# Attention of a 16-head language-model layer on one core: key projections one head ahead, a head finished at the end of the next one, fewer lower halves on VectorE, outputs read one unit later

## What is computed

```python
q = concat([q_nope, rope(q_rope)])                      # from nq = rms(x @ w_cq)
a1 = attn(q, k1, v1, causal=True)                       # LATENT: keys from ckv
a2 = attn(q, ks, vs, causal=False)                      # SELECT: 64 selected tokens
kw = (x @ w_wink); kw = concat([kw[:NOPE], rope(kw[NOPE:])])
a3 = attn(q, kw, vw, causal=True)                       # WINDOW
out = (g0 * a1 + g1 * a2 + g2 * a3) @ w_proj
```

## Time and profile before

| what | value |
|---|---|
| median of 3 runs | 2679.42 us (2678.9 to 2685.21) |
| the profiled execution | 2683.18 us, its span 2681.2 us |
| PE, DVE, ACT, POOL busy | 84%, 70%, 64%, 62% of the span |
| one head with preps (head 9), both halves | 68.91 us and 49.53 us |
| one head without preps (head 13), both halves | 59.19 us and 49.55 us |

### The profile page before, as it was taken

How to read it: one execution, slowest core, us unless ns; L and a number is a source line. 1 busy time by engine, 2 the same in 40 slices (tenths; PEclk the granted TensorE clock), 3 DMA queues, 4 the chain that set the end, 5 groups by cost and what they waited for, 6 DMA issues and landing times. The chain is left out here.

```text
span 2681.2 us, 37397 instructions
## 1 busy us (share of the span) xinstructions
PE 2243.5 (84%) x11394; PEld 1845.2 (69%) x11394; DVE 1868.2 (70%) x3832; ACT 1713.2 (64%) x3574; POOL 1655.0 (62%) x1432
## 2 busy tenths in 40 slices
...
PEclk9985569999999999999999999999999997759998
...
GB/s 383 325 190 248 200 101 138 81 83 126 37 141 44 140 67 112 104 59 116 64 142 47 136 85 78 66 64 66 60 40 62 21 30 50 170 55 189 211 193 171
DMA packets 199861, 314.81 MB, mean 117 GB/s; under 512 B 95916, under 2 KB 130220, under 8 KB 186732
## 3 DMA queue, kind: packets, MB, share of 16 engines
...
HBM read 210.20 MB, written 101.75 MB: 116 GB/s over the span
## 5 line engine op out<-in xcount | busy, mean ns | idle before, releaser
L1396 POOL TENSOR_TENSOR p_lo<-prob,p_hi 128x512 fp32r<-128x512 f32 (+2 forms) x960 | 1119.3, 1176 | 550.8 <-ACT p_hi L1480 516.9
L1478 ACT ACTIVATE prob<-ps_s 128x512 f32<-128x512 f32 (+4 forms) x1344 | 728.8, 542 | 432.2 <-DVE ps_s L1714 352.4
L1480 ACT ACTIVATE p_hi<-ps_s 128x512 fp32r<-128x512 f32 (+3 forms) x1344 | 729.8, 543 | 1.6
L1612 DVE TENSOR_REDUCE max_part<-ps_x 128x1 f32<-128x512 f32 x744 | 506.2, 686 | 51.8 <-PE ps_x L1524 44.0
L1396 DVE TENSOR_TENSOR p_lo<-prob,p_hi 128x512 fp32r<-128x512 f32 (+1 forms) x320 | 261.2, 816 | 13.0 <-ACT p_hi L1480 11.6
L1610 DVE CUSTOM_DVE_ANT_0 ps_x<-ps_x,before 128x128 f32<-128x128 f32 x496 | 243.6, 493 | 25.4 <-PE ps_x L1524 17.1
L1577 PE MATMUL ps_o<-p_hi,v_win 128*128 128x512 f32 (+3 forms) x640 | 237.5, 371 | 5.6 <-DVE p_lo L1396 5.6
L1714 DVE TENSOR_TENSOR ps_s<-ps_s,mask_kq 128x128 f32<-128x128 f32 x512 | 152.7, 301 | 126.1 <-PE ps_s L1496 120.2
L1577 PE MATMUL ps_o<-p_hi,v_lat 128*128 128x512 f32 (+3 forms) x640 | 236.1, 369 | 0.1
L1579 PE MATMUL ps_o<-p_lo,v_win 128*128 128x512 f32 (+3 forms) x640 | 236.1, 369 | 0.0
L1579 PE MATMUL ps_o<-p_lo,v_lat 128*128 128x512 f32 (+3 forms) x640 | 234.4, 366 | 0.0
...
## 6 DMA issues: line engine op xcount, KB each, us to landing
...
```

The lines of the kernel that those rows point to most:

```text
L1396: ns.tensor_tensor(upper if low else p_lo[:, i % LSLOTS, c:CH], prob[low:P, i % NPROB, c:CH], upper.bitcast(F32), ALU.subtract).then_inc(s ...
L1478: nc.scalar.activation(prob[low:P, i % NPROB, c:CH], ps_s[i % 3][low:P, c:CH], ACT.Exp, scale=SCALE).then_inc(s["p_full"], 1)
L1480: nc.scalar.activation(p_hi[:, i % SLOTS, c:CH], ps_s[i % 3][:, c:CH], ACT.Exp, scale=SCALE).then_inc(s["p_up"], 1)
L1612: ins = nc.vector.tensor_reduce(mpart[:, q, c:c + 1], bank[:, 0:w], axis=AX.X, op=ALU.max)
```

## The change

Four edits to the attention:

1. `prep_tasks` and `schedule`: a head's three `q` preps stand at units 1, 5 and 9 instead of 1, 4 and 7. The three `kw` preps, which stood at 10, 13 and 16 of the same head, are moved to the head in front, to its units 48, 53 and 58. Head 0 keeps its own six and also takes those of head 1; head 11 has `q` alone. The loads and stores of `kw` move with them in SP's order, and the weights get a load each.
2. `FINISH`: the six steps of the head before stand at units 50, 76, 78, 79, 80 and 82. The store of the inverse, the load of the weights and the store of the output move to the end of SP's order.
3. `LO_DVE`: every sixth causal unit instead of every fourth, so 13 instead of 20 a head.
4. `OUT_LAG`: `dve_output` stands five units behind a row's end; ACT's `read_sums` stays at four.

The diff, cut to its core (what is left out renames the semaphore of the weights and the counters that follow the new order):

```diff
@@ -1024,9 +1024,9 @@
     return [("max", h, b, q, c) for j in js for q in range(4 * j, 4 * j + 4) for c in range(q // 4 + 1)]
-def prep_tasks(g, j):
-
-    return [("prep", g, what, j, part) for what in ("q", "kw") for part in range(3)]
+def prep_tasks(what, n):
+
+    return [("prep", n // NJ + 1, what, n % NJ, part) for part in range(3)] if n < NJ * (NG - 1) else []
 def schedule():
...
@@ -1038,8 +1038,11 @@
         for n, t in enumerate(tasks):
             at.setdefault((h, lo + n * (hi - lo) // len(tasks)), []).append(t)
     for h in range(H):
-        if h + 4 < H:
-            spread(h, prep_tasks(h // 4 + 1, h % 4), *((1, 19) if h else (6, 24)))
+        if h:
+            spread(h, prep_tasks("q", h), 1, 13)
+        else:
+            spread(h, prep_tasks("q", 0) + prep_tasks("kw", 0), 6, 24)
+        spread(h, prep_tasks("kw", h + 1), HU + 4, HU + 19)
         spread(h, max_tasks(h, LATENT, range(NJ)), 7 if h else 9, HU - 6)
         spread(h, [("neg", h, 0)], HU - 4, HU - 3)
         if h + 1 < H:
...
@@ -1053,19 +1056,22 @@
 XN = {t: n for n, t in enumerate(ALL_X)}
 NX = 3
 PREP = [t for t in ALL_X if t[0] == "prep"]
-OUTS = {t: n for n, t in enumerate(("out", g, what, j, r) for g in range(1, NG) for j in range(NJ) for what in ("q", "kw") for r in range(3))}
+BATCH = [t[1:4] for t in PREP if t[4] == 0]
+BN = {b: n for n, b in enumerate(BATCH)}
+OUTS = {("out",) + b + (r,): 3 * n + r for n, b in enumerate(BATCH) for r in range(3)}
 NO = 3
 LAST_MAX = {(t[1], t[2]): XN[t] for t in ALL_X if t[0] == "max"}
-XP = {t: n for n, t in enumerate(PREP)}
+WHAT_NO = {b: sum(c[1] == b[1] for c in BATCH[:n + 1]) for b, n in BN.items()}
 NEG = {t: n for n, t in enumerate(t for t in ALL_X if t[0] == "neg")}
 PIN = [(g, j) for g in range(1, NG) for j in range(NJ)]
 SPLIT_L, SPLIT_W = 20, HU + 16
 CAUSAL = [i for i in range(NU) if UNITS[i][0] != SELECT]
 DIAG = [i for i in CAUSAL if UNITS[i][2] >= 4 * UNITS[i][1]]
-LO_DVE = sorted(CAUSAL[2::4] + [i for i in range(NU) if UNITS[i][0] == SELECT])
+LO_DVE = sorted(CAUSAL[2::6] + [i for i in range(NU) if UNITS[i][0] == SELECT])
 LO_POOL = [i for i in range(NU) if i not in LO_DVE]
 PV_LAG = 4
+OUT_LAG = PV_LAG + 1
 SLOTS, LSLOTS = 6, 4
 NPROB = 3
...
@@ -1180,14 +1186,19 @@
         def low_done(eng, n):
-            m, k = divmod(n, 6)
-            eng.wait_ge(s["low_pool" if k else "low_dve"], 5 * m + k if k else m + 1)
+            own = lambda m: BATCH[m // 3][1] == "q" and m % 3 == 0
+            eng.wait_ge(s["low_dve" if own(n) else "low_pool"], sum(own(m) == own(n) for m in range(n + 1)))
         def full_free(eng, n):
-            n -= NO if n % 6 != 3 else 2 * NO
+            n -= NO
+            while n >= 0 and n % 3 == 0 and BATCH[n // 3][1] == "q":
+                n -= NO
             if n >= 0:
                 low_done(eng, n)
+
+        def batch(t):
+            return BN[t[1:4]]
         @block.sync
         def _(sp):
...
@@ -1237,16 +1248,20 @@
             def load_kw_inputs(n):
                 j = n % NJ
                 if n:
-                    sp.wait_ge(s["x_read"], XN[PREP[6 * n - 1]] + 1)
+                    sp.wait_ge(s["x_read"], XN["prep", PIN[n - 1][0], "kw", PIN[n - 1][1], 2] + 1)
                 sp.dma_start(in_u[:].bitcast(F32), g.ut_dram[j]).then_inc(s["in_kw"], 16)
                 sp.dma_start(in_t[:, 2:4, :].rearrange("p s c -> p (s c)"), g.tab_dram[j]).then_inc(s["in_kw"], 16)
                 sp.dma_start(in_t[:, 4, :], g.row_dram[0:1, j * CH:(j + 1) * CH].to_broadcast([P, CH])).then_inc(s["in_kw"], 16)
-            def load_weights(gr):
+            def load_wq(gr):
                 if gr > 1:
-                    sp.wait_ge(s["x"], XN[PREP[24 * (gr - 1) - 1]] + 1)
-                sp.dma_start(wq[:].rearrange("p s n -> p (s n)").bitcast(F32), g.wq_dram[gr]).then_inc(s["w"], 16)
-                sp.dma_start(wkw[:].rearrange("p s k n -> p (s k n)").bitcast(F32), g.wkw_dram[gr]).then_inc(s["w"], 16)
+                    sp.wait_ge(s["x"], XN["prep", gr - 1, "q", NJ - 1, 2] + 1)
+                sp.dma_start(wq[:].rearrange("p s n -> p (s n)").bitcast(F32), g.wq_dram[gr]).then_inc(s["w_q"], 16)
+
+            def load_wkw(gr):
+                if gr > 1:
+                    sp.wait_ge(s["x"], XN["prep", gr - 1, "kw", NJ - 1, 2] + 1)
+                sp.dma_start(wkw[:].rearrange("p s k n -> p (s k n)").bitcast(F32), g.wkw_dram[gr]).then_inc(s["w_kw"], 16)
             def store_out(gr, j, what, part):
                 n = OUTS[("out", gr, what, j, part)]
...
@@ -1327,30 +1343,25 @@
                     load_sums(h - 1)
                 if h and nxt:
                     load_ks(h + 1)
+                if ahead and h and j == 3:
+                    load_wkw(gr + 1)
                 if prep:
-                    if n < len(PIN):
-                        load_q_inputs(n)
+                    if ahead:
+                        load_q_inputs(h + 1)
                     store_out(gr, j, "q", 1)
                     store_out(gr, j, "q", 2)
-                if prep:
-                    store_out(gr, j, "kw", 0)
-                    if n < len(PIN):
-                        load_kw_inputs(n)
-                    store_out(gr, j, "kw", 1)
-                    store_out(gr, j, "kw", 2)
-                if h:
-                    store_inverse(h - 1)
-                    load_weight(h - 1)
-                if prep:
+                    if not h:
+                        store_out(gr, j, "kw", 0)
+                        load_kw_inputs(1)
+                        store_out(gr, j, "kw", 1)
+                        store_out(gr, j, "kw", 2)
                     if j == 3:
                         if gr + 1 < NG:
-                            load_weights(gr + 1)
+                            load_wq(gr + 1)
                         outputs_stored(gr)
                         load_q(h + 1)
                         load_kw(h + 1, 0)
-                if h:
-                    store_output(h - 1)
-                else:
+                if not h:
                     load_ks(1)
                 store_rows(h, 0)
                 store_sums(h, 2)
...
@@ -1358,8 +1369,19 @@
                     load_kw(h + 1, 1)
                     load_v(h + 1, WINDOW)
                 store_sums(h, 0)
+                if ahead:
+                    store_out(*PIN[h + 1], "kw", 0)
+                    if h + 2 < len(PIN):
+                        load_kw_inputs(h + 2)
+                    store_out(*PIN[h + 1], "kw", 1)
+                    store_out(*PIN[h + 1], "kw", 2)
+                if h:
+                    store_inverse(h - 1)
+                    load_weight(h - 1)
                 if nxt:
                     store_rows(h + 1, 1)
+                if h:
+                    store_output(h - 1)
             store_sums(H - 1, 1)
             load_sums(H - 1)
             store_inverse(H - 1)
...
@@ -1716,13 +1738,13 @@
                         dve_task(dve, t)
                     if i - 1 in LO_DVE:
                         lower(dve, h, i - 1)
-                    if back(h, i, PV_LAG):
-                        dve_output(dve, *back(h, i, PV_LAG))
+                    if back(h, i, OUT_LAG):
+                        dve_output(dve, *back(h, i, OUT_LAG))
                     if h and i in FINISH:
                         dve_finish(dve, h - 1, FINISH[i])
                 if NU - 1 in LO_DVE:
                     lower(dve, h, NU - 1)
-            for i in range(NU - PV_LAG, NU):
+            for i in range(NU - OUT_LAG, NU):
                 dve_output(dve, H - 1, i)
             for step in range(6):
                 dve_finish(dve, H - 1, step)

```

More of the change, by code:

```diff
@@ L1304, in _ @@
             load_k1(0)
-            load_weights(1)
+            load_wq(1)
+            load_wkw(1)
             load_q_inputs(0)
@@ L1312, in _ @@
                 prep = gr < NG
-                n = h + 1
                 nxt = h + 1 < H
                 same = nxt and (h + 1) % 4
+                ahead = h + 1 < len(PIN)
                 if h:
@@ L1374, in turn_sum @@
                 n = out_number(t, 1)
-                pool.wait_ge(s["turn"], XP[t] // 3 + 1)
+                pool.wait_ge(s["turn"], batch(t) + 1)
                 for r, (x, y, op) in enumerate(((0, 2, ALU.subtract), (1, 3, ALU.add))):
@@ L1439, in round_up @@
                 elif part == 0:
-                    act.wait_ge(s["full"], XP[t] // 6 + 1)
+                    act.wait_ge(s["full"], WHAT_NO[t[1:4]])
                     src = full[:, n % NO, :]
                 else:
-                    act.wait_ge(s["back"], 2 * (XP[t] // 3) + part)
+                    act.wait_ge(s["back"], 2 * batch(t) + part)
                     src = full[:, n % NO, :]
```

16 lines of the change are left out of this document (8 added, 8 removed).

## The result

| | before | after |
|---|---|---|
| median, us (4 runs each) | 2680.81 (2678.9 to 2685.21) | 2634.31 (2629.7 to 2636.5) |
| ratio | 1 | 0.9826 [0.9807, 0.9844] |
| span of the profiled execution, us | 2681.2 | 2634.8 |

The change is 46.5 us faster. I had predicted 2612, range 2572 to 2655, so the time lies in the range and 22 us above the forecast: some two thirds of the expected 67 us came.

The account below looks back on a forecast made before the run. PE bounds second halves nearly alone; DVE's queue order costs a fifth of first halves. Heads 1 to 10 -44, head 11 -10, heads 12 to 15 -16, head 0 +3: -67 from 2679.4 gives 2612 us, range 2572 to 2655.

Parts of the forecast that it names:

- Output a unit later: First halves: DVE's wait for low_sum goes, saving 3.9 us of the 7.9 lost (bounds 0 to 4.0 or more).
- First half of head 9: From 68.9 to 58.9 us, 10.0 less; includes 2.8 us of kw columns and 2.4 us of their stalls.
- the five finish operations at units 76 to 82: End of a head: they fall into DVE's idle time and cost nothing; up to 3.7 us without that cover.
- paragraph on the rule: DVE with two SBUF inputs and POOL exclude each other; finish operations would be held up where POOL is fullest.
- Second half of head 9: From 49.5 to 55.1 us, 5.6 more (range 3 to 9), with the kw products added.
- POOL's cluster at units 59 to 64: Second half: POOL falls 4.7 us behind, of which 2.3 us reach PE (0 to 4.7).
- DVE at units 48 to 56: Second half: added kw parts and a finish step just fit, DVE at 97%; costs 1.0 us (0 to 2).
- Three lower halves leave DVE: First half: DVE rid of 2.6 us; with the finish's leaving, 0.9 us less lost.
- the lead did not hide the cluster: Rival, chance 0.18: the lead hides POOL's cluster, second half only +3.3 us, total 2577 us.
- the `low_sum` wait did not stay: Rival, chance 0.10: the later read still waits, first halves keep 3.9 us more loss, total 2674 us.
- POOL did not bound the half: Rival, chance 0.09: POOL bounds the second half, units 49 to 66, 11.5 us more, total 2698 us.
- Units 40 to 43: First half: chain of maxima and transposition, part of the 4.0 us of loss left to stay.

Follow-up runs that it names:

- experiment 1: Kernel before with only the output read one unit later: 2647.28 us, ratio 0.9869.
- experiment 9: Changed kernel with the output read four units behind a row's end again: 2705.18 us, ratio 1.0092 against the kernel before.
- experiment 4: Kernel before with only the key (kw) projections moved one head ahead: 2702.28 us, ratio 1.0085.
- experiment 5: Changed kernel with the split of the next head's window values at units 70 and 72 instead of 60 and 62: 2603.83 us.
- Experiment 12: Kernel before with later output, fewer DVE lower halves and later finish, the key projections staying in their own head: 2616.2 us.
- experiment 11: Changed kernel with value split at units 70 and 72, finish at units 50 to 76, unit 62's lower half on DVE: 2589.09 us.
- experiment 7: Changed kernel with every fourth causal lower half on DVE again (20 instead of 13 a head): 2681.47 us.
- experiment 2: Kernel before with only seven lower halves a head moved from DVE to POOL: 2724.38 us, ratio 1.0175.
- experiment 8: Changed kernel with value split at units 70 and 72, finish back at units 20 to 35, unit 62's lower half on DVE: 2602.36 us.

## Why the prediction was right, and where its terms were off

**Output a unit later: right in place and mechanism.** I took 3.9 us for a first half. Experiments 1 and 9 show the wait of the earlier trace rows to be the cause. The size is that of the whole, not of the edit alone: heads 12 to 14 gained 4.0 us, but 2.6 with this edit alone (experiment 1), and they lose 3.6 to 3.7 without it (experiment 9). In the first half of head 9 it is 1.9 alone (68.91 to 67.0) and 4.8 in the whole (60.08 to 64.84).

**First half of head 9: -10.0 predicted, -8.8 measured.** The missing 1.2 us is the term of the five finish operations at units 76 to 82, which the sum has at *"nothing"*. I read the cover from DVE's idle time and took the duration from the old place. But the operations have two SBUF inputs and now run beside POOL's densest row: additions of 1.6 to 1.8 instead of 0.69 us, multiplications of 0.8 to 1.5, together 3.5 us a head beyond their undisturbed time, before 0.6. That overran into the next head's masks and cost 1.5 us at units 0 to 4. The prediction named this in its paragraph on the rule and did not put it into the sum. The term belongs at 1.5, within the bound of 3.7 that it had; the rest of the first half came out 0.3 better than forecast, though DVE was busy 49.0 us and not the 46 of the prediction.

**Second half of head 9: +5.6 predicted, +6.4 measured, with the terms otherwise.** By units, measured: 2.8 us of columns, 4.0 more lost at units 63 to 72, 0.4 more at 53 to 57, 0.75 less at 44 to 47: 6.4. POOL's cluster at units 59 to 64, *2.3 us*, was right: one wait of 2.16, and 2.45 us lost in unit 66. (POOL's load over the whole half was 43.9 us, not 47.1.) Not in the sum was what comes behind it: the lower granted clock, some 1.5 us a head (the two heads of experiment 4 differ by that; experiment 5, without the stall, is at 1.00 and 3.26 us shorter). DVE at units 48 to 56 got 1.0 in the sum and cost 0.4. Experiment 12 has the keys' move by itself: against it the changed kernel's first half of head 9 is 5.2 us shorter, as the terms 2.8 + 2.4 said, and its second half 7.1 longer, where 2.8 + 1.0 + 2.3 = 6.1 was predicted. So the move was a loss by these terms already, 0.9 us a head, and became 1.9. My sentence that a granted clock other than 1.00 *"is not the change's"* was wrong: the change made the stall behind which it fell, in ten heads of ten.

**The sum.** 1.2 and 0.8 us over ten heads are 20 us. Heads 1 and 5, which I had counted as head 9, gave 6.7 of it back: 5.4 because they were at a lower clock before (121.85 and 120.45 us), 1.3 because head 1 has no finish in front of it now. The 5.4 are luck. Head 0 adds 2.6, head 11 0.4, head 15 3.1, and the stretches ahead of and behind the attention 1.5 (its first scores come 3.1 later, its end to the span's 1.6 sooner, 431.8 for 433.4). Before rounding that makes 20.6, the difference between the expected 67 and the spans' 46.4.

**Head 11: -10 predicted, -9.6 measured. Heads 12 to 14: -4, and -4.0. Head 15: -4, and -0.9.** Its first half gained 3.7 us and its second lost 2.9. The loss is at the very end. From the last unit's scores to the end of its values it took 5.99 us, before 2.72: POOL makes nine lower halves in a row, PE waits three times for one (0.37, 0.94 and 0.75 us), and from 2198 to 2203 the granted clock is 0.71. POOL and the second and third of these waits:

```profile
2189.51 12.26 POOL L1418 TENSOR_TENSOR p_lo<-prob,p_hi 128x512 fp32r<-128x512 f32 x9
...
2199.74 0.50 PE L1599 MATMUL ps_o<-p_hi,v_lat 128*128 128x512 f32 x1 [0.94 <-POOL p_lo L1418]
...
2201.41 0.79 PE L1599 MATMUL ps_o<-p_hi,v_lat 128*128 128x512 f32 x1 [0.75 <-POOL p_lo L1418]
```

The finish of head 14 beside that row is part of it: in experiment 11, which has it earlier, the nine take 10.63 us, two waits of 0.5 us stay, and the half is 46.8 us, after 48.1, before 45.2.

**Head 0: +3 predicted, +5.6 measured.** I gave its first half -2.5; it got 1.1 slower. Units 0 to 14 gained 4.1 us, but units 15 to 19 lost 2.9, by the same lockout at unit 17, and 20 to 43 another 2.2. The changed kernel, DVE, POOL, ACT:

```profile
418.66 4.46 DVE L1418 TENSOR_TENSOR p_lo<-prob,p_hi 128x512 fp32r<-128x512 f32 x1
...
417.53 2.55 POOL L1408 TENSOR_TENSOR st_lo<-full,st_hi 128x512 fp32r<-128x512 f32 x2
420.04 2.53 POOL L1418 TENSOR_TENSOR p_lo<-prob,p_hi 128x512 fp32r<-128x512 f32 x2
...
424.80 0.49 ACT L1500 ACTIVATE prob<-ps_s 128x384 f32<-128x384 f32 x1 [4.28 <-DVE ps_s L1736]
```

Units 15 to 19 of head 0 lose 4.18 us, before 1.31.

**"Three lower halves leave DVE ... 0.9 us": the size hid a sign.** I costed the edit by load. Alone it costs 47 us, in the whole it gives 47. Alone, some 36 us are lower halves of DVE that start into an unbroken row of POOL; in the whole such lockouts explain at most 13, and the rest lies elsewhere (experiment 7). My price per operation from its mean duration has neither, and that the total came out in the range with this term so far off is partly luck.

**Rivals.** None came in full: the lead did not hide the cluster (PE waits), the `low_sum` wait did not stay, and POOL did not bound the half. Of the lines that I named, these held: `low_sum` under 40 us, mask waits down (by 41%, I had a third), halves of 60.1, 56.0 and 55.9 us for 59, 55 and 55.5, PE's values waiting for `p_lo`.

**Units 40 to 43.** In the changed kernel 1.7 us stay there (before, 2.4). I had put that down to the chain of the maxima. Most of it is no wait but PE's own work, 16 narrow products for SELECT's maxima, here in the kernel before:

```profile
1528.26 0.97 PE L1520 MATMUL ps_x<-ks_hi,head_first 96*128 96x64 f32 x8
1529.07 0.48 PE L1577 MATMUL ps_o<-p_hi,v_win 128*128 128x512 f32 x1
```

Eight of 64 columns take 0.81 us, so both groups take 1.62, where the count by columns gives them 0.46.

**Open.** Some 11 of the 47 us of experiment 2. By the traces, 4.8 are in units 5 to 14 of heads 1 to 15 and 5.4 in units 20 to 43 of heads 12 to 15; the `low_sum` waits were still in place there, and I did not separate them. (The prediction's "78% to 82%" for DVE's share of the first halves is 81% and 82% by the earlier trace rows; no term goes by it.)

## What to carry to other kernels

Look first for an in-order engine that waits for one thing with others queued behind it: one slot in its order was worth 35 us alone and 71 in the whole, the largest gain of the four. Before work is moved to another engine or place, read what the engine that it excludes does *there*: a duration is that of its place, and an engine's unbroken row can hold up the other's one operation for 3 to 5 us. And try each edit both alone and left out of the whole: here two changed sign between the two, and the moved key projections cost 18 us while a single split stood beside them.

## What the runs showed of the chip

- **DVE can wait until POOL pauses.** A DVE operation with two SBUF inputs, 0.69 us by itself, took 3.95, 4.46 and 5.73 us, and each time it ended 0.55 us after the end of an unbroken row of POOL operations. It got no turn between two of them. The changed kernel's attention has 320 such operations 512 wide: 149 were not held and took 0.69 us, 146 ended behind the end of one POOL operation, 24 behind that of a second (2.47 us at unit 17 of heads 1 to 11), one behind that of a fourth; the kernel before has 267, 153, 12 and none. Each that was held ended 0.55 to 0.62 us behind the last of those ends. How many it lets pass is not explained by any run. Where ACT waits for a mask behind DVE's operation it makes nothing new for POOL, and so POOL's row comes to its end: in experiment 7 POOL's next operation, at 1459.86, comes after 1.53 us without work, when ACT has made the next upper half.
- **What it cost.** What such DVE operations took beyond their undisturbed 0.69 us (0.43 where 256 wide) sums to 78 us over the attention before and 131 after (53 of it the finish's multiplications and additions, 9 before): the changed kernel wins in spite of it.
- **One stall of 2.16 us, and the lower clock behind it.** In 3.00 us PE was busy 1.39, and the granted clock of the next stretch was 0.55. Where the stall was gone (experiments 5, 8, 11 and 12) the second halves of heads 1 to 10 stayed at 1.00. In experiment 4 the same order of work drew the lower level in some heads and not in others.
- **Spread.** Experiment 7 lay between 2653 and 2691 us over ten runs, and in its profiled one the second halves of heads 1 to 10 show granted clocks from 0.92 to 1.00; the others stay within 16 us. That stalls behind which the clock sometimes falls make the time uneven fits this, but only one run of it was profiled.
